# Sums of a gated image in two buffers over all images, its maxima kept twice, and two small products of TensorE in each other's place

## The chip, the cores and the metric

The kernel runs on one core of a Trainium2 chip. The metric is the device time of one execution, in microseconds (us).

## What is computed

The input is 16 images of 112 by 112 pixels with 256 channels in float32. Two layers follow each other; in each the input is normalised in 32 groups of 8 channels and a branch is added.

```python
# layer 0: group norm, signs, depthwise 3x3 convolution with signs of the kernel
x = x + _L0_conv_ref(_gn(x), L0_conv_kernel)
# layer 1, on g = _gn(x)
x = x + _L1_conv_ref(_gn(x), ...)
...
avg = jnp.mean(x, axis=(1, 2))
mx = jnp.max(x, axis=(1, 2))
fc = lambda v: jax.nn.relu(v @ ca_w1.T) @ ca_w2.T
ca_gate = jax.nn.sigmoid(fc(avg) + fc(mx))[:, None, None, :]
xc = x * ca_gate
m = jnp.mean(xc, axis=-1, keepdims=True).reshape(Bn, H * W, 1)
y = _s6(m, A, d_w, d_b, B_w, B_b, C_w, C_b).reshape(Bn, H, W, 1)
feat = jnp.concatenate([mean over channels of xc, max over channels of xc], axis=-1)
s = lax.conv_general_dilated(feat, lsa_w, ...)
x2 = xc * sigmoid(y) + xc * sigmoid(s)
out = relu(batch norm of x2)
```

What matters here: for each image the channel gate needs the whole image's mean and maximum after layer 0 (two small matrix products, a relu between them, an exponential behind them), and the gated image then needs, per pixel, its mean and its maximum over the 256 channels.

## The kernel before

The work is three stages. The first goes through the 16 images and does layer 0, the statistics and the channel gate, and the two per-pixel features. The second (state scan, spatial convolution) and the third and fourth passes over the images come behind it; the change leaves them alone but for the place of one small tile.

**Layout.** Channels lie on the 128 partitions in two halves (`j`), pixels along the free axis. An image is cut into 14 units of 896 pixels for one half (`NP = 14`, a unit has an upper and a lower part), and 28 tiles of 896 pixels by 128 channels (`NTILE = 28`). Each engine has its own loop `image(i)` with 14 steps `h`, written out in program order; each engine works through its list in order, and semaphores alone tie the lists together. Semaphores count over all images, so a wait such as `gexp_in >= i` names one event.

**TensorE**, `image(i)` from L1424. A step is 18 tap products of the depthwise convolution of unit `h` (L1440), nine for each half of the unit's rows. Steps 0 and 1 need extra products for a row above (L1447). Between the taps two tiles of the next image are turned from pixels on partitions to channels on partitions (`turn_tile`, L1316 to L1340, seven transposes into PSUM region `tile_ps`), and behind them come, for strip `c` of the image before, the means over channels (`channel_sums`, L1373), and the turning back of the maxima (`blocks_back`, L1387). A strip runs behind the convolution: step `h` handles strip `h - 5` of image `i - 1`, or, where that is negative, the last strips of image `i - 2`. Small products share the upper part of `tile_ps`: `group_sums` (L1344) at the end of an image, `stat_sums` (L1350) in step 0, `hidden` (L1356) at the end of step 1, `gate` (L1362) behind it, after the sums and turned blocks of step 1. `turn_tile(i + 1, 1)` stands in the middle of step 1, `turn_tile(i + 1, 2)` after five taps of step 2. `max_rows` (L1400) turns the partial maxima of image `i - 2` in step 5.

**ScalarE**, `image(i)` from L906. In a step it moves two turned tiles from PSUM to SBUF (`evacuate`, L835, each with a sum), packs the convolution's result (`pack`, L843), squares a finished unit for the variance (`square`, L851), multiplies a strip by its channel gate (`apply_gate`, L882 and L886) and moves the sums of a strip out (`average`, L900). `hidden` (L865) and `gate_exp` (L869) stand in step 1, `max_rows` (L893) in step 5. `evacuate(i + 1, 1)` stands in step 0.

**VectorE**, `image(i)` from L1230. In a step: the signs of a unit two steps ahead (`make_signs`, L1057 and L1071; from step 2 on at the step's start), the maximum of a strip's two channel halves (`max_halves`, L1209), the maxima of the turned blocks (`reduce_blocks`, L1220), the convolution added to the unit (`add_convolution`, L1122, two instructions), and in strips 2 to 9 the second half of the gate's multiplication (`gate_half`, L1199). `gate_argument` (L1178) stands at the start of step 1, `image_gate` (L1185 to L1189) at the end of step 2. At an image's start it also does the sums and statistics (L1039 to L1049, L1111 to L1169).

**SyncE's queue**, `image(i)` from L720: per step the load of a pair of tiles, the store of a finished unit, the load of a strip for the gate, and the store of a strip pair's sums (`sums_out`, L678).

Three waits matter.

```python
# TensorE, turn_tile, L1332 to L1335
if n == 1 and i >= 2:
    pe.wait_ge(shift_made, i - 1)
if n == 2 and i >= 2:
    pe.wait_ge(gexp_in, i - 1)
# ScalarE, average, L896 and L899: b = c // 2 % 2, over 7 strip pairs
act.wait_ge(sum_out[b], i * (16 * turns(b, 2, NS)) + 16 * (s // 2) + 1)
```

Called for image `i + 1`, the second of them says that tile 2 is not turned before VectorE has read the gate products of image `i - 1` out of the same PSUM region. Seven strip pairs are odd, so the last pair of one image and the first of the next use the same buffer of `srow`, and the average of the next image's first strip waits for the store of the last. `reduce_blocks` of strip 0 (L1216) waits until the maxima of the image before are turned.

Of the kernel before, what the change touches and what calls it, by code (L numbers as in the profile page):

```python
# [5 lines left out]
def binary_conv_then_gated_ssm_block(  # L6
# [30 lines left out]
    ACT = mybir.ActivationFunctionType  # L37
    AX = mybir.AxisListType.X

    P = 128  # L40
# [43 lines left out]
    with ctx:  # L84
# [72 lines left out]
        bnsum = sb("bnsum", [P, NB, 2 * NJ])  # L157
        pmax = sb("pmax", [P, 2 * NS * TG])
        pmax_rows = sb("pmax_rows", [2 * NS * TG, P])
# [161 lines left out]

        rows_ps = max_ps[1][0:2 * NS * TG, 384:384 + P]

# [324 lines left out]
        with nc.Block() as block:  # L648
            @block.sync
            def _(sp):  # L650
# [27 lines left out]
                def sums_out(i, s):  # L678
                    sp.wait_ge(averaged, i * NP + 2 * s + 2)
                    sp.dma_start(feat_d[0, i, s * SP:(s + 1) * SP].rearrange("(a q n) -> q a n", a=2, q=4),  # L680
                                 srow[s % 2][0:P:32, :, :]).then_inc(sum_out[s % 2], 16)

# [17 lines left out]
                def first_group(h):  # L700

                    if h == 0:
                        sp.wait_ge(turned, NB * NTILE)
                        sp.wait_ge(feats_out, 16 * GI + 1)
                        for b in range(2):
                            sp.wait_ge(sum_out[b], 16 * GI * turns(b, 2, NS) + 1)
                        sp.dma_start(bands_flat, bands_d).then_inc(bands_in, 16)
                        sp.wait_ge(pads_made, 2)
                        load_features(sp, 0)
                    if h == 2:  # L710
                        for j in range(NJ):
                            sp.wait_ge(stored[NU - 1][j], 16 * (NB - 1))
                        sp.wait_ge(squared, (NB - 1) * NP)
                        load_m(sp, 0, px[0][0])
                    if h == 11:
                        for k, t, n in ((2, 4, 6), (1, 3, 7), (0, 2, 8)):
                            sp.wait_ge(delta_steps, n)
                            store_px(sp, 0, k, px[0][t])
# [48 lines left out]
                for b in range(2):  # L767
                    sp.wait_ge(sum_out[b], NB * 16 * turns(b, 2, NS) + 1)

# [50 lines left out]
            def _(act):  # L820
# [69 lines left out]
                def max_rows(i):  # L890
                    act.wait_ge(rows_turned, i + 1)
                    act.wait_ge(feats_out, i * 16 + 1)
                    nc.scalar.activation(pmax_rows[:, :], rows_ps, ACT.Identity).then_inc(rows_made, 1)  # L893

                def average(i, c):
                    s, b = c // 2, c // 2 % 2  # L896
                    act.wait_ge(summed, i * NP + c + 1)
                    if c % 2 == 0:
                        act.wait_ge(sum_out[b], i * (16 * turns(b, 2, NS)) + 16 * (s // 2) + 1)  # L899
                    nc.scalar.activation(srow[b][:, c % 2, :], sum_ps(c), ACT.Identity).then_inc(averaged, 1)  # L900
# [5 lines left out]
                def image(i):  # L906
                    first, more, channels = i == 0, i + 1 < NB, i >= 1
                    for h in range(NP):
                        u, j = divmod(h, NJ)
                        last = h == NP - 1  # L910
                        if 2 <= h < NP - 1 and more:
                            evacuate(i + 1, 2 * h - 2)
                        if last and more:
                            evacuate(i + 1, NTILE - 3)
                        if h == 5 and i >= 2:
                            max_rows(i - 2)
                        pack(i, h, first)
                        if last and more:
                            evacuate(i + 1, NTILE - 2)
                            evacuate(i + 1, NTILE - 1)  # L920
                        if h == 1 and channels:
                            hidden(i - 1)
                        if (at := strip_at(i, h, 5)) and h >= 1:
                            average(*at)
                        if h >= 2 and not last and more:
                            evacuate(i + 1, 2 * h - 1)
                        if h == 0 and more:
                            evacuate(i + 1, 1)
                        if h >= 1:
                            square(i, (h - 1) // NJ, (h - 1) % NJ, first)  # L930
                        if h == NP - 2 and more:
                            evacuate(i + 1, NTILE - 4)
                        if last:
                            if i + 2 < NB:
                                evacuate(i + 2, 0)
                            square(i, NU - 1, 1, first)
                            if more and channels:
                                average(i - 1, 9)
                        if at := strip_at(i, h, 3):
                            apply_gate(*at)  # L940
                        if h == 1 and channels:
                            gate_exp(i - 1)
                        if i == NB - 1 and h == 6:
                            delta_exp(act, 0)
                        if i == NB - 1 and h == 8:
                            delta_log(act, 0)

                    inverse_deviation(i)
# [34 lines left out]
            def _(dve):  # L983
# [228 lines left out]
                def reduce_blocks(i, c):  # L1212

                    if c == 0:
                        if i >= 1:
                            dve.wait_ge(rows_turned, i)  # L1216
                    for q in range(2):
                        t0, t1 = 4 * q, min(4 * q + 4, TG)
                        dve.wait_ge(max_turned, i * NRED_STEPS + 2 * c + q + 1)
                        nc.vector.tensor_reduce(pmax[:, c * TG + t0:c * TG + t1],  # L1220
                                                max_ps[q][:, 0:(t1 - t0) * P].rearrange("p (t c) -> p t c", c=P),
# [8 lines left out]
                def image(i):  # L1230
                    more, channels = i + 1 < NB, i >= 1
                    for h in range(NP):
                        u, j = divmod(h, NJ)
                        if h == 1 and channels:
                            gate_argument(i - 1)
                        if h >= 2 and u + 2 < NU:
                            make_signs(i, u + 2, j)
                        if at := strip_at(i, h, 4):
                            max_halves(*at)
# [73 lines left out]
            def _(pe):  # L1313
                pe.wait_ge(consts_made, 2)

                def turn_tile(i, n):  # L1316
# [13 lines left out]
                    else:  # L1330
                        pe.wait_ge(evacuated, i * NTILE + (n if n < NTILE - 1 else NTILE - 2))
                        if n == 1 and i >= 2:  # L1332
                            pe.wait_ge(shift_made, i - 1)
                        if n == 2 and i >= 2:
                            pe.wait_ge(gexp_in, i - 1)  # L1335
                    ring = turned_ps(n) if i else first_ring[n % 3]
                    for t in range(TG):
# [40 lines left out]
                def blocks_back(i, c):  # L1378

                    pe.wait_ge(maxed, i * NP + c + 1)  # L1380
                    for q in range(2):
                        if c == 0 and i >= 1 and q == 1:
                            pe.wait_ge(rows_made, i)
                        if c >= 1:
                            pe.wait_ge(reduced, i * NRED_STEPS + 2 * c + q - 1)
# [12 lines left out]
                def max_rows(i):  # L1398
                    pe.wait_ge(reduced, i * NRED_STEPS + NRED_STEPS)
                    nc.tensor.transpose(rows_ps, pmax[:, :], ident[:, :]).then_inc(rows_turned, 1)  # L1400

# [22 lines left out]
                def image(i):  # L1424
# [5 lines left out]
                    for h in range(NP):  # L1430
# [12 lines left out]
                        if u == 0:  # L1443
                            for t in range(9):
                                tap(0, t)
                                if t < 3:
                                    nc.tensor.matmul(turn[h % 2][:, 0:W], taps[:, j, t, :], above[:, t:t + W],  # L1447
                                                     start=False, stop=False)
                                if t == 5 and more and (h == 1 or first):
                                    turn_tile(i + 1, h)  # L1450
# [5 lines left out]
                        else:  # L1456
                            for t in range(9):
                                if t == 5 and h == 5 and i >= 2 and more:
                                    max_rows(i - 2)
                                if t == 5 and not more:  # L1460
                                    spatial(h)
                                if t == (3 if h == last else 5) and more:
                                    turn_tile(i + 1, 2 * h - 2)
# [5 lines left out]
                        if h == 1 and channels:  # L1469
                            if more:  # L1470
                                pe.wait_ge(evacuated, (i + 1) * NTILE + 2)
                            hidden(i - 1)
# [8 lines left out]
                        if at:  # L1481
# [3 lines left out]
                            else:  # L1485
# [3 lines left out]
                                blocks_back(*at)  # L1489
                        if h == 1 and channels:  # L1490
                            gate(i - 1)
                        if 2 <= h < last and more:
# [80 lines left out]
        g2_p = scratch[:, :].bitcast(fp32)[:, G0 + NB * NS * NJ:G0 + 2 * NB * NS * NJ].rearrange("p (n j o) -> p n j o", n=2 * NS, j=NJ)  # L1573
        wsum = sb("wsum", [P, NB, 2 * NJ])
        bn = sb("bn", [P, 12, NJ])
# [453 lines left out]
```

## Time and profile before

| | |
|---|---|
| median of 3 runs | 3325.71 us (3324.7 to 3326.61) |
| span of the profiled execution | 3373.7 us (no other time of that execution is given) |
| TensorE, weight loads, VectorE, ScalarE busy | 2587.4, 1657.5, 2976.3, 2701.0 us |
| HBM traffic | 805.14 MB read, 420.17 MB written |

All times below are of the profiled execution, counted from its first instruction. An image is taken from one `group_sums` product (L1344) to the next. PE is TensorE, PEld its weight loads, DVE VectorE, ACT ScalarE, POOL GpSimd, SPq SyncE's queue. PEclk is the granted clock of TensorE, 1.00 for 2.4 GHz and 0.50 for 1.2 GHz. In a row of the timeline the first number is the start, the second the duration of the merged group, and a bracket gives the idle time of that engine just before and who ended it.

### The profile page before, as it was taken

The numbers are of one execution on the slowest core, as the hardware profiler recorded it, in microseconds if no ns is written. First come the engines' busy times: TensorE is split into PE (matmuls) and PEld (weight loads), VectorE is DVE, ScalarE is ACT, GpSimd is POOL, SyncE is SP. The second block draws the span as 40 slices with busy tenths as digits, with TensorE's granted clock in tenths as the row PEclk, the third lists the DMA queues.
The fourth block names the chain that finished last, engine by engine and source line by source line (L and its number), as shares of the span: only waits on it lengthen the run. The fifth ranks groups of instructions, "written<-read, shape, count | busy, mean of one in ns | idle before, by whom it ended". The sixth has DMA issues, their size and how long they took to land. (4 is left out here: it accounts for less than half of the span.)

```text
span 3373.7 us, 50742 instructions
## 1 busy us (share of the span) xinstructions
PE 2587.4 (77%) x17105; PEld 1657.5 (49%) x17105; DVE 2976.3 (88%) x4060; ACT 2701.0 (80%) x3772; POOL 56.8 (2%) x111
## 2 busy tenths in 40 slices
PE   7899999999999999999976333333776776766676
PEld 5566666666566666665432000000555555555555
DVE  8788999889998889988886999998999899888787
ACT  6788888888888888887763888887888888877777
POOL 3000000000000000000001100000000000000000
PEclk9999999999999999999986555555877778777767
DMA  8899999999999999998755999996999999999997
GB/s 318 328 374 399 386 367 366 364 368 401 374 364 365 369 398 384 366 367 335 274 129 122 380 420 419 420 421 261 382 428 430 428 426 420 415 386 374 373 369 289
DMA packets 199056, 1227.97 MB, mean 364 GB/s; under 512 B 29792, under 2 KB 38936, under 8 KB 157644
## 3 DMA queue, kind: packets, MB, share of 16 engines
q1 hardware_dynamic: 195884, 1223.41, 91.1%
q0 software_dynamic: 2976, 2.00, 0.3%
q8 instruction: 117, 1.92, 0.2%
q14 instruction: 79, 0.65, 0.0%
HBM read 805.14 MB, written 420.17 MB: 363 GB/s over the span
## 5 line engine op out<-in xcount | busy, mean ns | idle before, releaser
L1440 PE MATMUL psum<-signs,taps 128*128 128x448 f16 x4032 | 855.4, 355 | 29.4 <-DVE signs L1071 14.4
L1554 PE MATMUL psum<-signs,picked 12*128 12x448 bf16 x896 | 334.4, 517 | 340.4 <-DMA signs<-gate_scratch 276.6
L1945 ACT ACTIVATE stage<-psum 128x512 f32<-128x512 f32 x784 | 407.5, 614 | 209.1 <-DMA out_dram<-stage 186.7
L1440 PEld LDWEIGHTS psum<-signs,taps 128*128 128x128 f16 x4032 | 386.8, 98 | 351.7 <-issue 33.8
L1965 DVE SCALAR_TENSOR_TENSOR xc<-xt,curs,psum 128x1792 f32<-128x1792 f32 x222 | 452.0, 2077 | 121.7 <-PE psum L1554 119.2
L835 ACT ACTIVATE xt<-psum 128x896 f32<-128x896 f32 x416 | 378.0, 910 | 151.8 <-PE psum L1338 128.0
L1757 DVE SCALAR_TENSOR_TENSOR xc<-xt,curs,psum 128x1792 f32<-128x1792 f32 x224 | 455.8, 2077 | 34.0 <-PE psum L1554 33.1
L1691 ACT ACTIVATE xc<-xc 128x1792 f32<-128x1792 f32 x224 | 380.0, 1697 | 95.9 <-DVE xc L1757 95.9
L1122 DVE CUSTOM_DVE_ANT_0 xt<-scratch,xt 128x896 f32<-128x896 int8 x416 | 435.7, 1084 | 14.2 <-ACT scratch L843 14.2
L1338 PE MATMUL psum<-ident,stage 128*128 128x128 f32 x3066 | 410.2, 276 | 16.4 <-DMA stage<-x_dram 10.6
L1933 ACT ACTIVATE xc<-xc,bn,curs 128x1792 f32<-128x1792 f32 x224 | 411.1, 1899 | 7.6 <-DVE xc L1965 4.2
L1910 PE MATMUL psum<-ident,last_unit 128*128 128x128 f32 x1568 | 288.0, 355 | 157.2 <-ACT stage L1945 129.3
L1910 PE MATMUL psum<-ident,signs 128*128 128x128 f32 x1568 | 285.8, 353 | 141.1 <-ACT stage L1945 123.4
L851 ACT ACTIVATE hsum<-xt,mean 128x1792 bf16<-128x1792 f32 x208 | 370.2, 1780 | 23.8 <-DVE x1max_p L1122 23.8
L1338 PEld LDWEIGHTS psum<-ident,stage 128*128 128x128 f32 x3066 | 354.5, 143 | 63.6 <-issue 24.2
L1554 PEld LDWEIGHTS psum<-signs,picked 12*128 12x128 bf16 x896 | 87.5, 118 | 548.8 <-DVE xc L1757 379.8
L1910 PEld LDWEIGHTS psum<-ident,last_unit 128*128 128x128 f32 x1568 | 255.3, 213 | 202.0 <-ACT stage L1945 167.1
L1910 PEld LDWEIGHTS psum<-ident,signs 128*128 128x128 f32 x1568 | 254.6, 212 | 186.8 <-ACT stage L1945 155.7
L1209 DVE TENSOR_TENSOR stage<-xc 128x896 f32<-128x896 f32 x224 | 243.8, 1088 | 67.5 <-ACT xc L882 54.1
L1220 DVE TENSOR_REDUCE pmax<-psum 128x4 f32<-128x512 f32 x448 | 257.7, 617 | 50.9 <-PE psum L1387 45.3
L1071 DVE SCALAR_TENSOR_TENSOR signs<-xt,mean,signs 128x896 f16<-128x896 f32 x208 | 240.3, 1155 | 7.4
L843 ACT ACTIVATE scratch<-psum,border 128x896 int32<-128x896 f32 x224 | 223.8, 999 | 21.1 <-PE psum L1440 21.0
(222 smaller groups left out, 2830.4 us busy)
## 6 DMA issues: line engine op xcount, KB each, us to landing
xt<-x_scratch SPq DMA_DIRECT2D x210, 1792.0 KB
out_dram<-stage SPq DMA_DIRECT2D x112, 1792.0 KB, 13.6
stage<-x_dram SPq DMA_DIRECT2D x219, 896.0 KB, 9.0
xc<-x_scratch SPq DMA_DIRECT2D x210, 896.0 KB, 8.2
x_scratch<-xt SPq DMA_DIRECT2D x208, 896.0 KB, 8.5
x_scratch<-last_unit SPq DMA_DIRECT2D x16, 896.0 KB, 8.9
signs<-ssm_scratch SPq DMA_DIRECT2D x14, 448.0 KB, 4.6
xc<-ssm_scratch SPq DMA_DIRECT2D x14, 448.0 KB, 5.0
```

The source lines that it names most:

```text
L835: nc.scalar.activation(dst, src, ACT.Identity, scale=XL if part else 1.0, accum_out=xsum_p[:, j, 2 * u + part:2 * u + part + 1]).then_inc( ...
L851: nc.scalar.activation(squares.rearrange("p (a n) -> p a n", a=2), unit(i, j, u), ACT.Square, scale=-1.0, bias=mean0[:, i % 2, j:j + 1], a ...
L1122: nc.vector.tensor_tensor_reduce(out=px, in0=conv, in1=px, scale=1.0 / XL if part else 1.0, scalar=-3.0e38, op0=ALU.add, op1=ALU.max, accu ...
L1338: ins = nc.tensor.transpose(ring[:, t * P:(t + 1) * P], xin[b][:, t, j * P:(j + 1) * P], ident[:, :])
L1440: return nc.tensor.matmul(turn[h % 2][:, b * 512:b * 512 + HB], taps[:, j, t, :], signs[:, j, r:r + RT // 2, dw:dw + W], start=t == 0, sto ...
L1554: last = nc.tensor.matmul(dst[:, b, :], picked[:, b * P:(b + 1) * P], gate_rows[:, s * BW:(s + 1) * BW], start=True, stop=True)
L1691: nc.scalar.activation(u, u, ACT.Square, accum_out=g2_p[:, n, j, bass.ds(it, 1)]).then_inc(squared3, 1)
L1757: nc.vector.scalar_tensor_tensor(quarters(xc[n % 2][:, j, :]), slot_quarters(s, j), curs[:, h, j:j + 1], gate_quarters(gate_ps3[n % 2]), A ...
L1910: last = nc.tensor.transpose(out_ps[k % 4][:, v * C + j * P:v * C + (j + 1) * P], block_in, ident[:, :])
L1933: nc.scalar.activation(u, u, ACT.Relu, bias=bn[:, 7, j:j + 1], scale=curs[:, h, NJ + j:NJ + j + 1]).then_inc(relu_made, 1)
L1945: nc.scalar.activation(outs[n % 2][:, 2 * k:2 * k + 2, :].rearrange("p t c -> p (t c)"), out_ps[k % 4], ACT.Identity).then_inc(staged, 1)
L1965: nc.vector.scalar_tensor_tensor(quarters(xc[n % 2][:, j, :]), slot_quarters(s, j), curs[:, h, j:j + 1], gate_quarters(gate_ps4), ALU.add, ...
```

## The change

Average buffers: the buffer of a strip pair's sums is chosen by the pair's number over all images. Partial maxima: `pmax` gets two copies, one for odd and one for even images; they are turned in step 6, no longer in step 5, and into the free end of `tile_ps`. Gate products: on TensorE `gate` goes from the end of step 1 to behind three tap pairs of step 2; `turn_tile(i + 1, 1)` takes its place at the end of step 1; tile 2 is turned behind seven tap pairs, no longer five. VectorE's `gate_argument` goes from the start of step 1 to step 2, behind `make_signs`; ScalarE's `gate_exp` from the end of step 1 to the start of step 2, its `evacuate(i + 1, 1)` from step 0 to step 1. A tile of the batch norm, `wsum`, is laid over one that is free by then.

```diff
-        pmax = sb("pmax", [P, 2 * NS * TG])
+        pmax = sb("pmax", [P, 2, 2 * NS * TG])
...
-        rows_ps = max_ps[1][0:2 * NS * TG, 384:384 + P]
+        def rows_ps(i):
+
+            if i < NB - 3:
+                return tile_ps[0:2 * NS * TG, TP:TP + P]
+            return max_ps[1][0:2 * NS * TG, 384:384 + P]
...
-                                 srow[s % 2][0:P:32, :, :]).then_inc(sum_out[s % 2], 16)
+                                 srow[(i * NS + s) % 2][0:P:32, :, :]).then_inc(sum_out[(i * NS + s) % 2], 16)
...
                 def average(i, c):
-                    s, b = c // 2, c // 2 % 2
+                    g = i * NS + c // 2
+                    b = g % 2
                     act.wait_ge(summed, i * NP + c + 1)
                     if c % 2 == 0:
-                        act.wait_ge(sum_out[b], i * (16 * turns(b, 2, NS)) + 16 * (s // 2) + 1)
+                        act.wait_ge(sum_out[b], 16 * (g // 2) + 1)
...
                         last = h == NP - 1
+                        if h == 2 and channels:
+                            gate_exp(i - 1)
                         if 2 <= h < NP - 1 and more:
                             evacuate(i + 1, 2 * h - 2)
...
-                        if h == 5 and i >= 2:
+                        if i >= 2 and h == (6 if more else 5):
                             max_rows(i - 2)
...
-                        if h == 0 and more:
+                        if h == (1 if channels else 0) and more:
                             evacuate(i + 1, 1)
...
-                        if h == 1 and channels:
-                            gate_exp(i - 1)
...
-                    if c == 0:
-                        if i >= 1:
-                            dve.wait_ge(rows_turned, i)
+                    if c == 0 and i >= 2:
+                        dve.wait_ge(rows_turned, i - 1)
...
-                        if h == 1 and channels:
-                            gate_argument(i - 1)
                         if h >= 2 and u + 2 < NU:
                             make_signs(i, u + 2, j)
+                        if h == 2 and channels:
+                            gate_argument(i - 1)
...
                         if n == 1 and i >= 2:
                             pe.wait_ge(shift_made, i - 1)
+                            pe.wait_ge(hid_in, i - 1)
                         if n == 2 and i >= 2:
                             pe.wait_ge(gexp_in, i - 1)
+                        if n == 11 and i >= 3:
+                            pe.wait_ge(rows_made, i - 2)
...
-                        if c == 0 and i >= 1 and q == 1:
+                        if c == 0 and i >= NB - 2 and q == 1:
                             pe.wait_ge(rows_made, i)
-                        if c >= 1:
+                        if i >= 1 or c >= 1:
                             pe.wait_ge(reduced, i * NRED_STEPS + 2 * c + q - 1)
...
-                                if t == 5 and more and (h == 1 or first):
+                                if t == 5 and more and first:
                                     turn_tile(i + 1, h)
...
-                                if t == 5 and h == 5 and i >= 2 and more:
+                                if t == 5 and h == 6 and i >= 2 and more:
+                                    pe.wait_ge(evacuated, (i + 1) * NTILE + 2 * h - 2)
                                     max_rows(i - 2)
...
-                                if t == (3 if h == last else 5) and more:
+                                if t == 3 and h == 2 and channels:
+                                    if more:
+                                        pe.wait_ge(evacuated, (i + 1) * NTILE + 2)
+                                    gate(i - 1)
+                                if t == (3 if h == last else 7 if h == 2 else 5) and more:
                                     turn_tile(i + 1, 2 * h - 2)
...
                             if more:
-                                pe.wait_ge(evacuated, (i + 1) * NTILE + 2)
+                                pe.wait_ge(evacuated, (i + 1) * NTILE + 1)
                             hidden(i - 1)
...
-                        if h == 1 and channels:
-                            gate(i - 1)
+                        if h == 1 and channels and more:
+                            turn_tile(i + 1, 1)
...
-        wsum = sb("wsum", [P, NB, 2 * NJ])
+        assert 2 * NJ * NCNT == NB * 2 * NJ
+        wsum = weighted[:, :, :, :].rearrange("p j a k -> p (j a k)").rearrange("p (b k) -> p b k", k=2 * NJ)
```

## Rows read from the trace of the kernel before

**Rows 1.** The page: busy time of the engines and its share of the span.

```profile
PE 2587.4 (77%) x17105; PEld 1657.5 (49%) x17105; DVE 2976.3 (88%) x4060; ACT 2701.0 (80%) x3772; POOL 56.8 (2%) x111
```

**Rows 2.** Windows: 13 images of the loop, and the start of image 11.

```profile
core 0: us, PE busy (x) PEld busy (x) DVE busy (x) ACT busy (x) POOL busy (x), PEclk, DMA share, GB/s
220.74:1564.69 1343.95, 1276.76 (x10257) 822.47 (x10257) 1221.98 (x2353) 1159.21 (x1808) 1.78 (x2) 1.00 0.94 374
...
1152.19:1177.10 24.91, 22.28 (x176) 13.34 (x176) 23.39 (x54) 19.82 (x33) 0.00 (x0) 1.00 0.78 282
```

**Rows 3.** Timeline of TensorE, image 11, steps 2 to 7.

```profile
1167.70 0.60 PE L1362 MATMUL psum<-hid,w 16*128 16x1 f32 x4 [1.09 <-ACT hid L865]
1168.23 2.08 PE L1440 MATMUL psum<-signs,taps 128*128 128x448 f16 x10
1170.15 0.93 PE L1338 MATMUL psum<-ident,stage 128*128 128x128 f32 x7
1170.92 1.69 PE L1440 MATMUL psum<-signs,taps 128*128 128x448 f16 x8
...
1175.52 2.08 PE L1440 MATMUL psum<-signs,taps 128*128 128x448 f16 x10 [0.24 <-ACT hsum L900]
...
1192.35 0.32 PE L1400 MATMUL psum<-ident,pmax 128*98 128x128 f32 x1 [0.69 <-DVE pmax L1220]
...
1198.09 2.07 PE L1440 MATMUL psum<-signs,taps 128*128 128x448 f16 x10 [0.57 <-ACT hsum L900]
...
1204.86 1.31 PE L1440 MATMUL psum<-signs,taps 128*128 128x448 f16 x6
```

**Rows 4.** Timeline of VectorE, image 11, around the gate's argument.

```profile
1167.17 1.08 DVE L1122 CUSTOM_DVE_ANT_0 xt<-scratch,xt 128x896 f32<-128x896 int8 x1
...
1169.20 0.15 DVE L1178 TENSOR_SCALAR st<-psum 128x2 f32<-128x2 f32 x1
1169.58 1.09 DVE L1209 TENSOR_TENSOR stage<-xc 128x896 f32<-128x896 f32 x1 [0.22 <-DVE st L1178]
...
1177.46 1.08 DVE L1209 TENSOR_TENSOR stage<-xc 128x896 f32<-128x896 f32 x1
```

**Rows 5.** Timeline of ScalarE, image 11, steps 0 to 6.

```profile
1163.56 0.92 ACT L835 ACTIVATE last_unit<-psum 128x896 f32<-128x896 f32 x1 [2.06 <-DMA x_scratch<-last_unit]
...
1169.32 1.79 ACT L851 ACTIVATE hsum<-xt,mean 128x1792 bf16<-128x1792 f32 x1 [1.43 <-DVE x1max_p L1122]
...
1182.57 0.92 ACT L835 ACTIVATE xt<-psum 128x896 f32<-128x896 f32 x1 [0.32 <-DMA x_scratch<-xt]
...
1189.45 0.92 ACT L835 ACTIVATE xt<-psum 128x896 f32<-128x896 f32 x1
...
1197.59 0.36 ACT L900 ACTIVATE hsum<-psum 128x224 f32<-128x224 f32 x1 [1.36 <-DMA feat_scratch<-hsum]
```

**Rows 6.** Waits from 220 to 1565 us: total, times, longest.

```profile
ACT hsum L900 <- DMA feat_scratch<-hsum: 11.7, 12, 2.4
PE psum L1440 <- ACT hsum L900: 9.6, 27, 1.4
PE psum L1400 <- DVE pmax L1220: 7.0, 13, 1.0
DVE st L1178 <- PE psum L1362: 1.9, 3, 1.2
```

**Rows 7.** Timeline of TensorE behind a long idle time in image 1.

```profile
150.46 1.73 PE L1338 MATMUL psum<-ident,stage 128*128 128x128 f32 x7 [3.14 <-ACT xt L835]
151.98 3.19 PE L1440 MATMUL psum<-signs,taps 128*128 128x448 f16 x8
155.08 1.54 PE L1338 MATMUL psum<-ident,stage 128*128 128x128 f32 x7
```

**Rows 8.** Windows of the same place and of image 6, columns as in rows 2.

```profile
149.00:156.00 7.00, 5.54 (x20) 3.46 (x21) 3.24 (x6) 6.51 (x9) 0.00 (x0) 0.53 1.02 425
646.00:651.00 5.00, 3.52 (x28) 2.33 (x29) 4.41 (x9) 4.58 (x9) 0.00 (x0) 0.68 0.04 17
```

More of the change, by code:

```diff
@@ L705, in first_group @@
                         for b in range(2):
-                            sp.wait_ge(sum_out[b], 16 * GI * turns(b, 2, NS) + 1)
+                            sp.wait_ge(sum_out[b], 16 * turns(b, 2, GI * NS) + 1)
                         sp.dma_start(bands_flat, bands_d).then_inc(bands_in, 16)
@@ L767, in _ @@
                 for b in range(2):
-                    sp.wait_ge(sum_out[b], NB * 16 * turns(b, 2, NS) + 1)
+                    sp.wait_ge(sum_out[b], 16 * turns(b, 2, NB * NS) + 1)
             @block.gpsimd
@@ L892, in max_rows @@
                     act.wait_ge(feats_out, i * 16 + 1)
-                    nc.scalar.activation(pmax_rows[:, :], rows_ps, ACT.Identity).then_inc(rows_made, 1)
+                    nc.scalar.activation(pmax_rows[:, :], rows_ps(i), ACT.Identity).then_inc(rows_made, 1)
                 def average(i, c):
-                    s, b = c // 2, c // 2 % 2
+                    g = i * NS + c // 2
+                    b = g % 2
                     act.wait_ge(summed, i * NP + c + 1)
                     if c % 2 == 0:
-                        act.wait_ge(sum_out[b], i * (16 * turns(b, 2, NS)) + 16 * (s // 2) + 1)
+                        act.wait_ge(sum_out[b], 16 * (g // 2) + 1)
                     nc.scalar.activation(srow[b][:, c % 2, :], sum_ps(c), ACT.Identity).then_inc(averaged, 1)
@@ L1219, in reduce_blocks @@
                         dve.wait_ge(max_turned, i * NRED_STEPS + 2 * c + q + 1)
-                        nc.vector.tensor_reduce(pmax[:, c * TG + t0:c * TG + t1],
+                        nc.vector.tensor_reduce(pmax[:, i % 2, c * TG + t0:c * TG + t1],
                                                 max_ps[q][:, 0:(t1 - t0) * P].rearrange("p (t c) -> p t c", c=P),
@@ L1399, in max_rows @@
                     pe.wait_ge(reduced, i * NRED_STEPS + NRED_STEPS)
-                    nc.tensor.transpose(rows_ps, pmax[:, :], ident[:, :]).then_inc(rows_turned, 1)
+                    nc.tensor.transpose(rows_ps(i), pmax[:, i % 2, :], ident[:, :]).then_inc(rows_turned, 1)
                 def spatial(h):
```

## The prediction

> **What bounds the kernel now.** The page comes first: none of the engines is full over the 3373.7 us [rows 1], but that is an average over unlike stages. The change touches only the loop over the images, so the windows by stage come next. From the first sums of image 2 to those of image 15, 13 images take 1343.95 us, 103.4 us each; TensorE is busy 95% of it at the full clock of 2.4 GHz (PEclk 1.00), VectorE 91%, ScalarE 86%, and the DMA engines 94% [rows 2]. Nearly bound by everything: there the order of the work decides.
>
> Then the timeline of one image. Image 11 is ordinary. In its later half TensorE goes through a step every 6.77 us (step 6 starts at 1198.09, step 7 at 1204.86) with nothing in a bracket [rows 3]; fourteen such steps are 94.8 us. The other 8.6 us of an image lie at its start. There the reader should look at VectorE, for it is the engine that is late. From 1152.19, right behind the group sums, to 1177.10 it is busy 23.39 of 24.91 us, and the remainder is hand-overs between small dependent instructions, as the 0.22 us behind L1178 [rows 2, 4]. It works with nobody to wait for; it reaches its step 1 at 1169.20, when TensorE is already in its step 2 (from 1168.23) [rows 3, 4]. So VectorE is a whole step behind TensorE here, and anything that TensorE must get out of VectorE's list is early or late by its place in that list.
>
> **The change, part by part**, on image 11.
>
> *The gate's argument.* Before, it is VectorE's first instruction of step 1 and runs at 1169.20. Tile 2 may be turned only after it, and is turned at 1170.15 [rows 3, 4]: a tight fit, without a wait. After the change it stands behind the whole of step 1 and the signs of step 2. Those end where the next `max_halves` starts before, at 1177.46. Without the argument and its hand-over in step 1 (1169.58 − 1169.20 = 0.38) they end at 1177.1, the argument is read at 1177.25, and TensorE gets the word at about 1177.4. Nothing brings that forward: all that VectorE does from 1152.19 to there stays in its list, and it was not waiting.
>
> *TensorE's step 2.* The end of step 1 gains. `hidden` no longer stands behind the evacuation of tile 1, and the 1.09 us that `gate` waits for ScalarE's relu are covered by sums and blocks [rows 3]. But step 2 needs signs that VectorE makes just before its addition at 1167.17 [rows 4], so it starts at 1167.25 where it started at 1168.23. Fourteen taps (18 take 2.08 + 1.69 us [rows 3], so 2.7) and the gate products (0.60) bring it to tile 2 at 1170.5. There it must wait until 1177.4: **6.9 us idle**, with the four last taps, the strip's sums and blocks and tile 3 behind it. Tile 2 takes 0.93, four taps 0.8; step 2's taps end at 1179.1, where they ended at 1172.6 (1170.92 + 1.69). That is 6.5 us late.
>
> *ScalarE.* `gate_exp` now heads step 2, where ScalarE arrives when step 1's gate multiplications are done, about 4 us before the word at 1177.4. It waits until then, with tile 2's evacuation and the packing of step 2 queued behind it [rows 5]. Those need TensorE's late results anyway, so this wait hides under TensorE's. The 2.06 us that ScalarE waited for a store in front of tile 1 go, but they bring nothing: its square was waiting 1.43 us for VectorE right after [rows 5], and VectorE is not earlier.
>
> *What is won back* before step 6. ScalarE paces steps 3 to 5 with 6.88 us each (1182.57 to 1189.45 [rows 5]); TensorE's 0.24 us waits for it go. Of the 6.5 us, 6.3 are left at step 3, 6.2 at step 5. In step 5 the turning of the maxima waited 0.69 us for VectorE and step 6 0.57 us for the average, itself 1.36 us late by the store of the same buffer [rows 3, 5]. With two copies and alternating buffers both waits are gone. Step 6 starts at 1202.65 where it started at 1198.09: 4.6 us late. The transpose of the maxima (0.32, about 0.2 of it beyond the stream [rows 3]) now falls into step 6. From there every engine is shifted alike, so **4.8 us per image** stay.
>
> *The clock.* Behind 3.14 us of idle time TensorE runs at half clock: a tile takes 1.73 us where rows 3 have 0.93, eight taps 3.19 for 1.69, the next tile 1.54, together 2.9 us more; the window holds 0.53 of the clock [rows 7, 8]. In image 6 a shorter gap leaves 0.68 over 5 us, which is 5 × 0.64 = 3.2 us at 1.2 GHz and some 1.6 us lost [rows 8]. An idle time of 6.9 us is longer than either, so I expect the fall in every image. No trace shows how long it lasts behind such a gap; the ends are nothing and 2.9 us, and I take 2.3, between the two cases seen. By the Trainium skill, "TensorE: Matmul & The Clock Gate", section "HAM oscillation — how this bites in real kernels", the penalty is the throttled time times one half; for the stretch in image 1 that is 3.3 us against the 2.9 in its rows, and by it the sum would be some 5 us higher over the loop.
>
> The same page, section "Step-by-step: what each phase is for", says that only weight loads are pulled ahead and matmuls stay in order. No row here shows a product slipping past a waiting one.
>
> *The rest at nothing, and why.* Turning tile 1 now waits for the relu. The gate products waited 1.09 us for it at the same place, since ScalarE came late from its 2.06 us at the store [rows 3, 5]; with that wait gone the relu is earlier, and were it not, up to 1 us would hide under the wait for the signs at 1167.25. The new wait of tile 11 for ScalarE's copy of the maxima comes behind eight taps, the sums and the blocks of the step in which they are turned, some 4 us. On SyncE's queue the same loads and stores are issued; those behind tile 3 come 6 us later, but so do their users, and the DMA engines, 94% busy, get slack. The second copy and the moved `wsum` issue nothing new.
>
> *Sum.* Images 2 to 14: 13 × (4.8 + 2.3) = 92 us. Image 1 has no strips in these steps, so VectorE comes some 5 us sooner and the stall is about 4 us; but image 1 also has the 3.14 us wait for a store and the half clock behind it [rows 7], which a later TensorE no longer meets: +1. Image 15 turns no tiles and is VectorE's anyway: 0. The later stages: 0. So +93 us on the profile's 3373.7. The median of the runs is 3325.71, 48 us below that span; the terms are waits within a stage paced by the engines, so I put them on the median unscaled: **3419 us**.
>
> **The rivals.**
> *A, the stall without the clock.* For it: 27 short waits of TensorE for the average left the clock at 1.00 [rows 2, 6]. Against: both longer gaps did not [rows 8]. 3325.7 + 13 × 4.8 + 1 = 3389 us.
> *B, faster.* VectorE reaches the moved argument before TensorE reaches tile 2. Then only the removed waits count. In the 13 images TensorE waited 7.0 us at the maxima and 9.6 us for averages [rows 6]; that gives 3325.7 − 16.6 = 3309 us. The point from which it decides: VectorE must be there by 1170.5, with 24.9 us of work that starts at 1152.19 [rows 2]; it misses by 6.7 us. For it speaks only that VectorE waited for the gate in three images (1.9 us [rows 6]), so it is not always the last.
> *C, worse.* The half clock lasts through steps 2 and 3, so that two long stretches as in image 1 follow each other (5.8 us): 13 × (4.8 + 5.8) = 138, 3465 us.
> *D, nothing.* The removed waits pay for the stall. They are 16.6 us in all against 13 × 6.5; it would take a stall of 1.3 us.
>
> **How the numbers follow.** Mine 0.60, A 0.22, B 0.05, C 0.10, D 0.03. The likeliest is 3419. The range takes in A with a few us below it for a smaller stall, and mine with 2.9 us of clock and a little of C: 3378 to 3445. A measurement of this kernel can tell about 0.2%, 7 us, from no change. Slower: mine, A and C, 0.92; the same 0.03; faster 0.05.
>
> **What would show it.** In the changed kernel's trace: images some 110 us apart, VectorE's L1178 some 25 us behind the image's mean (L1048 at 1152.19; 17 before) and never waiting for TensorE; a bracket of 6 to 7 us, released by VectorE, before the tile behind seven tap pairs of step 2; a bracket of some 4 us before ScalarE's exponential; PEclk of 0.5 once per image; no wait for the sums' store in front of step 6, and none of TensorE for the partial maxima. Wrong would be a tile 2 without a bracket, or images under 103 us apart; right in kind and off in size would be a clock that stays at 1.00.

## The result and the profile after

The changed kernel takes 3413.47 us (median of 4 runs, 3410.99 to 3418.8) against 3326.16 us for the kernel before: 1.0265 of it, with a 95% interval from 1.0251 to 1.0278, 87 us slower. The forecast was 3419 us. In this and the following sections a time given for a kernel is the median of all its executions, while a ratio leaves out the few of either kernel that took some 50 us longer, so that the two need not agree to the last digit.

Line numbers have moved: L1344 is L1351 now, the taps L1447, the turning of tiles L1345, `gate` L1369, the reading of the gate products L1183, ScalarE's exponential L873. The first view is the windows of the loop over images 2 to 14, with two places of image 11 (which starts at 1215.11) and one of image 9.

```profile
core 0: us, PE busy (x) PEld busy (x) DVE busy (x) ACT busy (x) POOL busy (x), PEclk, DMA share, GB/s
222.44:1655.88 1433.44, 1302.10 (x10258) 834.54 (x10258) 1227.92 (x2353) 1165.14 (x1808) 1.78 (x2) 0.96 0.91 351
1215.60:1240.40 24.80, 16.57 (x126) 9.24 (x118) 23.50 (x53) 16.03 (x25) 0.00 (x0) 0.93 0.78 283
1240.70:1244.20 3.50, 3.43 (x19) 2.16 (x23) 1.09 (x1) 1.34 (x4) 0.00 (x0) 0.54 0.81 330
1019.60:1025.60 6.00, 5.94 (x33) 3.66 (x34) 1.09 (x1) 2.53 (x5) 0.00 (x0) 0.51 0.48 193
```

The 13 images take 1433.44 us where they took 1343.95 [rows 2]: 110.3 us each, 6.9 more. VectorE and ScalarE have the same instructions and nearly the same busy time as before; only the time between them has grown. At the start of image 11 VectorE is busy 23.50 of 24.80 us, as in [rows 2], while TensorE falls from 22.28 to 16.57 us.

Then TensorE's timeline of image 11, steps 2 and 3, to be held against [rows 3].

```profile
1231.90 0.60 PE L1369 MATMUL psum<-hid,w 16*128 16x1 f32 x4
1232.44 1.70 PE L1447 MATMUL psum<-signs,taps 128*128 128x448 f16 x8
1240.77 1.73 PE L1345 MATMUL psum<-ident,stage 128*128 128x128 f32 x7 [6.64 <-DVEq L1184]
1242.29 1.70 PE L1447 MATMUL psum<-signs,taps 128*128 128x448 f16 x4
1243.92 0.96 PE L1380 MATMUL psum<-xc,over_c 128*32 128x224 f32 x16
```

Tile 2 waits 6.64 us, and what ends the wait is VectorE's queue at L1184, the word that the gate products have been read. Then the tile takes 1.73 us and four taps 1.70, nearly twice their time at full clock; at 1243.92 the clock is back. The other two engines at the same moment, VectorE first (with the image's mean, L1053, at the top):

```profile
1215.53 0.16 DVE L1053 TENSOR_SCALAR mean_low<-psum 128x2 f32<-128x2 f32 x1 [0.48 <-PE psum L1351]
...
1239.34 1.16 DVE L1076 SCALAR_TENSOR_TENSOR signs<-xt,mean,signs 128x896 f16<-128x896 f32 x1
1240.41 0.08 DVE L1076 DVE_READ_ACCUMULATOR signs<-xt,mean,signs 128x1 f32 x1
1240.41 0.15 DVE L1183 TENSOR_SCALAR st<-psum 128x2 f32<-128x2 f32 x1
1240.78 1.09 DVE L1214 TENSOR_TENSOR stage<-xc 128x896 f32<-128x896 f32 x1 [0.21 <-DVE st L1183]
1245.51 1.16 DVE L1224 TENSOR_REDUCE pmax<-psum 128x4 f32<-128x512 f32 x2 [3.63 <-PE psum L1394]
```

```profile
1235.47 1.12 ACT L890 ACTIVATE xc<-xc,gbias,par 128x896 f32<-128x896 f32 x1
1240.66 0.20 ACT L873 ACTIVATE st<-st 128x2 f32<-128x2 f32 x1 [4.07 <-DVEq L1184]
1242.62 0.92 ACT L839 ACTIVATE last_unit<-psum 128x896 f32<-128x896 f32 x1 [1.75 <-PE psum L1345]
```

The reading (L1183) starts the moment the signs are done, without a bracket: TensorE waits for VectorE, not the other way round. ScalarE stands 4.07 us before its exponential and then 1.75 us for the tile. The loss comes back on VectorE as 3.63 us of waiting for TensorE's blocks. The waits of the loop, in total, times and longest, to be held against [rows 6]:

```profile
PE psum L1345 <- DVEq L1184: 86.2, 13, 6.6
ACT st L873 <- DVEq L1184: 52.9, 13, 4.1
PE psum L1447 <- ACT hsum L905: 6.4, 26, 0.3
```

Thirteen stalls make 86.2 us. Neither the partial maxima nor the store of the sums is any longer what TensorE or ScalarE waits for in the loop.

### The profile page after: what moved, and what is told of

Read it like the earlier page. It is cut to its first block and busy times, and to the rows that moved or that the text cites. A ratio compares the mean times of both kernels' runs of the same rounds, so it can differ in the third digit from the quotient of the medians.

```text
span 3411.8 us, 50798 instructions
## 1 busy us (share of the span) xinstructions
PE 2582.0 (76%) x17105; PEld 1652.3 (48%) x17105; DVE 2981.6 (87%) x4060; ACT 2706.7 (79%) x3772; POOL 57.0 (2%) x111
## 5 line engine op out<-in xcount | busy, mean ns | idle before, releaser
L1447 PE MATMUL psum<-signs,taps 128*128 128x448 f16 x4032 | 866.8, 358 | 44.6 <-DVE signs L1076 31.9
L1447 PEld LDWEIGHTS psum<-signs,taps 128*128 128x128 f16 x4032 | 388.8, 99 | 373.5 <-DVE signs L1076 49.9
L1345 PE MATMUL psum<-ident,stage 128*128 128x128 f32 x3066 | 419.0, 280 | 107.2 <-DVEq L1184 89.8
L1345 PEld LDWEIGHTS psum<-ident,stage 128*128 128x128 f32 x3066 | 360.1, 144 | 155.7 <-issue 113.5
L1923 PE MATMUL psum<-ident,last_unit 128*128 128x128 f32 x1568 | 279.9, 348 | 143.5 <-ACT stage L1958 113.4
```

Of the source, the lines that this page charges most:

```text
L1345: ins = nc.tensor.transpose(ring[:, t * P:(t + 1) * P], xin[b][:, t, j * P:(j + 1) * P], ident[:, :])
L1447: return nc.tensor.matmul(turn[h % 2][:, b * 512:b * 512 + HB], taps[:, j, t, :], signs[:, j, r:r + RT // 2, dw:dw + W], start=t == 0, sto ...
L1923: last = nc.tensor.transpose(out_ps[k % 4][:, v * C + j * P:v * C + (j + 1) * P], block_in, ident[:, :])
```

## The experiments

**The kernel before, once more.** The profiled execution of before spanned 48 us more than its median run.

> The kernel before once more, for its trace. The profiled execution of before spans 3373.7 us, 48 us over the median of its runs. If that excess lies behind the image loop, a new trace shows the 13 images from 2 to 14 at 103.4 us each again and a span near 3325 us. If it lies inside the loop, the images are shorter than 103.4 us and the comparison of the two loops has to be made anew.

Measured: 3331.14 us, span 3329.4. Windows of the loop and of what follows, first in the second trace, then what follows in the first trace:

```profile
222.66:1568.29 1345.63, 1278.51 (x10257) 823.20 (x10257) 1222.51 (x2353) 1159.28 (x1808) 1.78 (x2) 1.00 0.94 374
1568.29:3329.40 1761.11, 1090.83 (x5523) 685.25 (x5523) 1575.29 (x1271) 1373.35 (x1689) 28.64 (x48) 0.71 0.91 368
```

```profile
1564.69:3373.70 1809.01, 1117.46 (x5523) 702.46 (x5523) 1575.68 (x1271) 1373.32 (x1689) 28.63 (x48) 0.70 0.90 358
```

The images are the same, 103.4 and 103.5 us each; the 48 us lie behind the loop (1809.01 against 1761.11 us). So the terms of the loop could rightly be put on the median unscaled.

**The reading put back.** In the changed kernel, on VectorE:

```diff
+                        if h == 1 and channels:
+                            gate_argument(i - 1)
                         if h >= 2 and u + 2 < NU:
                             make_signs(i, u + 2, j)
-                        if h == 2 and channels:
-                            gate_argument(i - 1)
```

> The changed kernel, with VectorE's reading of the gate products back at the start of its step 1; all else as changed. Theory (the place in VectorE's list makes the stall): TensorE reads on at once, no bracket before the tile behind seven taps, no half clock in images 2 to 14, and only the removed waits are left: 3309 us, 3300 to 3318. Rival (the stall comes from TensorE's own order, gate products and tile 1 changed over): it stays over 3380 us.

Measured: 3307.1 us, 0.994 of before (0.9919 to 0.9961); repeated 3306.23 us, 0.9947 (0.993 to 0.9964). TensorE and VectorE in image 11 and the loop's window:

```profile
1155.88 0.60 PE L1369 MATMUL psum<-hid,w 16*128 16x1 f32 x4
1156.41 1.70 PE L1447 MATMUL psum<-signs,taps 128*128 128x448 f16 x8
1157.95 0.93 PE L1345 MATMUL psum<-ident,stage 128*128 128x128 f32 x7
1156.52 0.16 DVE L1183 TENSOR_SCALAR st<-psum 128x2 f32<-128x2 f32 x1
```

```profile
221.64:1547.19 1325.55, 1277.14 (x10257) 820.68 (x10257) 1218.05 (x2353) 1159.68 (x1808) 1.78 (x2) 1.00 0.95 380
```

VectorE reads at 1156.52, tile 2 follows the taps with no bracket, and an image takes 102.0 us. ScalarE's exponential stands at the head of its step 2 here as in the changed kernel, so its place alone doesn't make the loss. One instruction of 0.15 us, moved by one step in one list, is 106 us of the difference between two kernels, and this one beats both.

**The reading at the head of step 2**, in front of the signs and no longer behind them.

```diff
+                        if h == 2 and channels:
+                            gate_argument(i - 1)
                         if h >= 2 and u + 2 < NU:
                             make_signs(i, u + 2, j)
-                        if h == 2 and channels:
-                            gate_argument(i - 1)
```

> The changed kernel, with the reading at the head of VectorE's step 2, in front of the signs, 1.85 us earlier. Theory (TensorE waits for exactly this instruction): the bracket falls from 6.6 to about 4.8 us, 13 x 1.85 = 24 us less, 3389 us; the half clock stays. If the stall had another releaser behind the reading, the time stays at 3413 us.

Measured: 3393.48 us (1.0197 of before, 1.015 to 1.0243).

```profile
1226.01 1.73 PE L1345 MATMUL psum<-ident,stage 128*128 128x128 f32 x7 [4.83 <-DVEq L1184]
1227.53 1.70 PE L1447 MATMUL psum<-signs,taps 128*128 128x448 f16 x4
1229.16 1.72 PE L1380 MATMUL psum<-xc,over_c 128*32 128x224 f32 x16
```

```profile
222.08:1639.03 1416.95, 1308.93 (x10257) 838.03 (x10257) 1228.33 (x2353) 1164.82 (x1808) 1.78 (x2) 0.97 0.93 355
```

The stall shrinks by 1.81 us, just the signs that changed sides. The images shrink by less, from 110.3 to 109.0 us: in this kernel the half clock lasts through the strip's sums (1.72 us for 0.96). Over the 8 us from the start of tile 2 the granted clock is 0.66 in the mean of its 13 images, where the changed kernel has 0.73. That is 1.1 us more at half clock. The forecast of 3389 us left the clock's part as it was and came out 4 us too low.

**The stall filled.** In the changed kernel, TensorE:

```diff
+                                if t == 7 and h == 2 and more and channels:
+                                    for _ in range(30):
+                                        nc.tensor.matmul(tile_ps[:, 0:HB], taps[:, j, 0, :],
+                                                         signs[:, j, u * RT:u * RT + RT // 2, 0:W], start=True, stop=True)
                                 if t == (3 if h == last else 7 if h == 2 else 5) and more:
                                     turn_tile(i + 1, 2 * h - 2)
```

> The changed kernel, with 30 extra products of TensorE into PSUM that nobody reads, in front of the wait for tile 2 in the images that turn tiles, some 5.7 us of work that fits into the 6.6 us stall. The output is unchanged. Theory (the fall of the clock is a cost of its own, 1.6 us per image by the changed kernel's rows): tile 2 takes 0.93 us again and the time falls by about 14 x 1.6 = 22 us to 3391 us. Rival (the half clock hides under other waits): 3413 us.

Measured: 3389.05 us (1.0179 of before, 1.0132 to 1.0226), 24 us faster than the changed kernel with 420 products more. Its timeline of image 11, `group_sums`, the end of step 2's wait, and the starts of steps 6 and 7 (L1476 are the extra products):

```profile
1199.36 0.38 PE L1351 MATMUL psum<-xsum,groups 128*128 128x2 f32 x2 [0.47 <-DVE xsum L1047]
...
1218.24 5.83 PE L1476 MATMUL psum<-signs,taps 128*128 128x448 f16 x30
1225.04 0.95 PE L1345 MATMUL psum<-ident,stage 128*128 128x128 f32 x7 [0.97 <-DVEq L1184]
1225.83 0.93 PE L1447 MATMUL psum<-signs,taps 128*128 128x448 f16 x4
...
1250.51 2.07 PE L1447 MATMUL psum<-signs,taps 128*128 128x448 f16 x10 [0.25 <-ACT hsum L905]
...
1257.38 2.08 PE L1447 MATMUL psum<-signs,taps 128*128 128x448 f16 x10
```

```profile
225.15:1632.34 1407.19, 1349.44 (x10648) 858.24 (x10648) 1228.42 (x2353) 1162.00 (x1808) 1.78 (x2) 1.00 0.93 358
```

The tile starts no earlier (25.7 us behind `group_sums` in both kernels), but at full clock. The loop takes 108.2 us an image, so of the 6.9 us lost, the clock is 110.3 − 108.2 = 2.0 and the wait itself 4.9. In image 1 the products are a loss: the changed kernel waits 3.55 us there with the clock at 1.00, and with the products image 2 starts 2.7 us later (225.15 against 222.44). The 13 images give 26 us, and image 1 takes 2.7 of them back.

**One part alone.** The kernel before with the reading behind the signs of step 2, and with ScalarE's exponential at the head of its step 2:

```diff
-                        if h == 1 and channels:
-                            gate_argument(i - 1)
                         if h >= 2 and u + 2 < NU:
                             make_signs(i, u + 2, j)
+                        if h == 2 and channels:
+                            gate_argument(i - 1)
```

> The kernel before, with one part of the change alone: VectorE's reading of the gate products behind the signs of its step 2 and ScalarE's exponential at the head of its step 2. Tile 2 still follows five taps. Theory (this one move makes the loss): a bracket of some 7 us before tile 2, eight taps behind it where the changed kernel has four (0.8 us more), and nothing won at the maxima and averages (about 1 us per image): 13 x (4.8 + 0.8 + 1.0 + 1.6) + 1 = 108 over before, 3433 us; 3410 to 3445. Rival (it needs the exchange of tile 1 and gate): within 10 us of before.

Measured: 3423.59 us, 1.0286 of before (1.026 to 1.0311), with the same releaser and 6.91 us before tile 2 of image 11:

```profile
1248.66 1.73 PE L1338 MATMUL psum<-ident,stage 128*128 128x128 f32 x7 [6.91 <-DVEq L1179]
```

The move alone costs more than the whole change. It came out 9 us under the forecast. (ScalarE's exponential, whose lines are not shown, moved with it; with the reading put back it did no harm at the same place.)

**ScalarE's exponential behind its step 2**, in the changed kernel.

```diff
-                        if h == 2 and channels:
-                            gate_exp(i - 1)
                         if 2 <= h < NP - 1 and more:
                             evacuate(i + 1, 2 * h - 2)
...
+                        if h == 2 and channels:
+                            gate_exp(i - 1)
                         if i == NB - 1 and h == 6:
```

> The changed kernel, with ScalarE's exponential behind all of its step 2 and no longer at its head. Theory (ScalarE's wait of 4.1 us hides under TensorE's): ScalarE waits for tile 2 in its place and the time stays, 3413 us within 5. Rival (ScalarE's wait delays the packing of step 2 and holds TensorE up): at least 13 us less, 3400 us or below.

Measured: 3416.5 us (1.0265 of before, 1.0239 to 1.0291): no change. ScalarE now waits 6.02 us for tile 2 in image 11, and the 4.07 us bracket was hidden under TensorE's, as the forecast had it.

**The average buffers alone**, in the kernel before.

```diff
-                    s, b = c // 2, c // 2 % 2
+                    g = i * NS + c // 2
+                    b = g % 2
                     act.wait_ge(summed, i * NP + c + 1)
                     if c % 2 == 0:
-                        act.wait_ge(sum_out[b], i * (16 * turns(b, 2, NS)) + 16 * (s // 2) + 1)
+                        act.wait_ge(sum_out[b], 16 * (g // 2) + 1)
```

> The kernel before, with the alternating average buffers alone. In the trace of before TensorE waits at step 6 for the average by 5.6 us in the 13 images: 3326 - 6 = 3320 us if each of these waits is on the path; 3326 us if VectorE, busy without a pause in these steps, is the bound.

Measured: 3320.84 us against 3329.47 beside it, 0.9969 (0.9954 to 0.9984), some 10 us by the ratio. That wait was on the path. The forecast had 6 us, and the loop of this trace (220.75 to 1558.74) is 6 to 8 us shorter than the two of before; the rest lies behind it.

**The maxima alone**: of the change, the two copies of `pmax`, their later turning and its new place.

```diff
-                                if t == 5 and h == 5 and i >= 2 and more:
+                                if t == 5 and h == 6 and i >= 2 and more:
+                                    pe.wait_ge(evacuated, (i + 1) * NTILE + 2 * h - 2)
                                     max_rows(i - 2)
```

> The kernel before with the doubled, later turned maxima alone. If TensorE's 7.0 us of waits at the maxima are on the path: 0.998 of before, no wait for the partial maxima in the trace. If the wait for the sums' store takes their place, the same as before, with a longer wait of ScalarE for that store in step 6's average.

Measured: 3327.39 us, 1.0003 of before (0.999 to 1.0015). Neither expectation is met cleanly. The wait for the maxima is gone from the waits; ScalarE's wait for the sums' store is there, but smaller than in [rows 6], not longer; TensorE's wait for the average has grown from 9.6 to 13.4 us, and five of the 13 images take over 105 us. (The traced execution took 3336.77 us, 9 us over the median, so it shows more long images than an ordinary one may have.)

```profile
PE psum L1445 <- ACT hsum L904: 13.4, 25, 1.6
ACT hsum L904 <- DMA feat_scratch<-hsum: 7.1, 8, 1.2
```

In image 6, one of the long ones, ScalarE waits 3.84 us for a store in front of tile 1, TensorE 2.41 us behind it, and then the taps of step 2 run at half clock, 3.72 us where [rows 3] have 2.08:

```profile
650.49 0.25 PE L1361 MATMUL psum<-fc_in,w 128*16 128x2 f32 x4 [2.41 <-ACT xt L839]
650.61 1.34 PE L1378 MATMUL psum<-xc,over_c 128*32 128x224 f32 x16
651.87 1.75 PE L1392 MATMUL psum<-ident,stage 128*128 128x128 f32 x7
653.57 1.00 PE L1367 MATMUL psum<-hid,w 16*128 16x1 f32 x4
654.50 3.72 PE L1445 MATMUL psum<-signs,taps 128*128 128x448 f16 x10
```

**Sums and maxima together**, so the whole change without the exchange of gate and tile 1.

> The kernel before, with the average buffers and the doubled, later turned maxima, and without the exchange of gate and tile 1. If the waits at the maxima (7.0 us) and at step 6 (5.6 us) are all that the change can win, this gives 3326 - 13 = 3313 us, and the kernel with the reading put back (3307 us) owes the remaining 6 us to the exchange. If the exchange gives nothing, both are equal, 3307 us.

> The kernel before with alternating average buffers and doubled maxima, a second time, beside the kernel with all parts and the reading put back. If the exchange of gate and tile 1 is worth something once the reading is early, this is some 6 to 10 us slower than the other (0.997 of before against 0.994). If not, both are equal.

> The changed kernel with the reading back at the start of VectorE's step 1, a second time, on one chip with the next kernel: 0.994 of before, as at first.

Measured: 3317.89 us, 0.9959 (0.9942 to 0.9977), and the second time 3309.72 us, 0.9948 (0.9935 to 0.9961), beside 3306.23 us, 0.9947, for the kernel with all parts and the early reading. The ratios don't separate the two, so on the time it stays open whether the exchange is worth anything. The traces lean one way: 103.0 and 102.7 us an image without it, 102.0 and 102.1 with it, and the waits of ScalarE in front of its evacuations differ, first without and then with the exchange (both with the early reading):

```profile
ACT xt L839 <- DMA x_scratch<-xt: 22.6, 10, 3.8
ACT last_unit L839 <- DMA x_scratch<-last_unit: 19.6, 8, 3.7
```

```profile
ACT xt L839 <- DMA x_scratch<-xt: 7.8, 9, 1.4
ACT last_unit L839 <- DMA x_scratch<-last_unit: 0.7, 1, 0.7
```

The long images go the same way. In the six traces without the exchange whose reading is early (the kernel before twice, the sums, the maxima, and both together twice), ten images of the loop take over 105 us. In each of them TensorE waits 1.8 to 2.4 us at `hidden` for ScalarE's evacuation of tile 1, and the granted clock falls to half. In the two traces with the exchange no image reaches 103 us, TensorE never waits over 0.7 us, and the clock stays at 1.00.

## Why the prediction was right, and where it was off

**The gate's argument.** Forecast: read 25 us behind the image's mean, by VectorE's own unbroken work, never waiting for TensorE. In image 11 it is 24.9 us behind it (1240.41 against 1215.53), with no bracket. That this one place makes the loss is shown from both sides: put back, the kernel is faster than before; moved alone (with ScalarE's exponential), it is slower by 2.9%; moved in front of the signs, the stall gives back just the signs' time.

**TensorE's step 2.** Forecast 6.9 us of idle time, measured 6.64. Step 2's start is paced by the signs, as said. Most of the difference is in the taps: the prediction gave fourteen of them 2.7 us, while 14/18 of the durations that it names (2.08 + 1.69) is 2.9.

**What is won back.** Forecast 4.8 us per image left without the clock; the filled kernel, which has the wait and not the half clock, shows 108.2 − 103.4 = 4.9. The way there is right too. In image 11 of the kernel before, `group_sums` stands here:

```profile
1151.77 0.38 PE L1344 MATMUL psum<-xsum,groups 128*128 128x2 f32 x2 [0.47 <-DVE xsum L1042]
```

From there to the start of step 6 (1198.09 in [rows 3]) it is 46.32 us, and in the filled kernel 51.15 us (1199.36 to 1250.51): 4.8 us more. To step 7 it is 4.9 us more. The forecast had 4.6 and 4.8.

**The clock.** Forecast 2.3 us per image between ends of nothing and 2.9; measured 2.0, and a cost of its own, since filling the gap pays 24 us. The clock falls in all 13 images, but for different times, though the wait is 6.63 or 6.64 us in each. In image 11 the granted clock is back after the tile and four taps; in image 9 the window from 1019.60 holds 0.51 of the clock over 6 us. Over the 8 us from the start of tile 2 the granted clock lies between 0.62 and 0.83, with 0.73 in the mean of the 13 images, which is 4.3 us at half clock. By "TensorE: Matmul & The Clock Gate", section "HAM oscillation — how this bites in real kernels" of the Trainium skill, half of the throttled time is lost. That makes an estimate of 2.1 us per image; the measured 2.0 agrees, and more closely than the 3.3 against 2.9 us of image 1 did.

**The sum.** By the start of image 15 the changed kernel is 91.2 us behind the first trace of before (1655.88 against 1564.69) and 87.6 us behind the second (1568.29), where the forecast had 93. From there on it is 5 us shorter than the second trace (1755.9 against 1761.1), which the forecast had at 0. These 5 us are not shown to belong to the moved waits of image 15: that stretch takes 1751.2 to 1759.1 us in the nine traces with the alternating average buffers, and 1760.1 to 1761.1 in the three without (the second of before, the move alone, the maxima alone). That points at the buffers, by single traces only.

**ScalarE's tile 1.** Here the step failed in part: "they bring nothing: its square was waiting 1.43 us for VectorE right after". In image 11 that is so. But the wait for that store differs from image to image, up to 3.8 us, and behind it TensorE stands at `hidden`, for 15.2 us in the 13 images of before, which no term and no rival of the prediction counts:

```profile
PE psum L1356 <- ACT xt L835: 8.0, 7, 2.3
PE psum L1356 <- ACT last_unit L835: 7.2, 6, 2.1
```

Where it stands there for some 2 us it can then work at half clock, as the rows of image 6 in the kernel with the maxima alone show. One ordinary image was read where the long ones decide. In the changed kernel this made no difference to the sum, whose part without the clock came out at 4.9 us for 4.8. That the late reading's stall covers these waits is argued, not shown by a run of its own.

**Rival B** named the right point: with the reading in time the kernel takes 3307 us where B had 3309. The 16.6 us that B put together were not the right ones, though, so that its number was met by luck. The sums and maxima bring the loop down by 5 to 11 us only (from 1343.95 and 1345.63 us to 1338.76 and, in the second trace, 1334.4), and the maxima alone bring nothing, because other waits take the place of theirs. By the traces a further 7 to 13 us of the loop come with the exchange (1325.55 and 1327.03 us), in which `hidden` no longer stands behind the evacuation of tile 1; the kernels' times don't confirm that part. B counted too much for the waits at maxima and averages and nothing for the exchange. Rivals A, C and D fell: the clock does fall, its fall costs less than 5.8 us, and the removed waits pay for only a part.

## What to carry to other kernels

Before moving an instruction within an engine's list, find how far behind that engine is at the place, in microseconds and not in steps: VectorE was a whole step late here, so that the reading, moved by one step, came 8 us later, and TensorE, which needed the same PSUM region, waited 6.6 us for it. A removed wait is worth what its long cases cost, so read it over all turns of the loop and not in the ordinary one. When TensorE must wait anyway, what follows the wait can run at half clock; count that too.

## What the runs showed beyond that

Extra work made a kernel faster: 30 products that nobody reads in each of 14 stalls, 420 in all, took 24 us off. It paid only where the clock fell: in image 1, with a wait of 3.55 us and the clock at 1.00, it cost 2.7 us. And a shorter stall was no cure for the clock. With 4.83 us instead of 6.64 the clock stayed low for longer, 5.4 us behind the wait in the mean of 13 images instead of 4.3, and of 1.8 us saved an image kept 1.3 (109.0 against 110.3 us). Half of the longer time at half clock, 0.6 us, is just what is missing.
